# Second mixture of experts: sixteen tiles instead of eight go through all experts on chip, in two sets

## What is computed

```python
logits = ln(t) @ gate_w + gate_b                     # 16 experts
top_probs, top_idx = top_k(softmax(logits), 2)       # two of them, shares normalized
h = silu(ln(t) @ w1[e]) * (ln(t) @ w2[e])            # 64 -> 128
t = t + sum over the two chosen e of share[e] * (h @ w3[e])   # 128 -> 64
```

## Time and profile before

| | |
|---|---|
| median of 3 runs | 960.18 us (952.63, 961.45, 960.18) |
| profiled execution | 959.24 us, span 957.1 us |
| busy share of the span | TensorE 68%, VectorE 59%, GpSimd 54%, ScalarE 30% |
| mean granted TensorE clock | 0.787 of full speed |
| `stage_mixture` of the second mixture | 693.8 to 881.4 us of the span |
| `stage_out` | 882.4 to 957.1 us |

### The profile page before, as it was taken

The page is one execution under the profiler, slowest core; times in us unless marked ns, Lnnn a source line. Parts: engine busy times, 40 slices in busy tenths (PEclk is TensorE's granted clock), DMA queues, the critical chain, the costliest instruction groups (busy, mean ns, idle before and its releaser), DMA issues. The chain is left out here.

```text
span 957.1 us, 12138 instructions
## 1 busy us (share of the span) xinstructions
PE 646.1 (68%) x3571; PEld 429.6 (45%) x3571; DVE 568.5 (59%) x1058; ACT 288.4 (30%) x556; POOL 517.4 (54%) x494
## 2 busy tenths in 40 slices
PE   3797875405239989989519953199455998930893
PEld 2795863404223257767413443134243776720222
DVE  6468575597796523545676558854574553510685
ACT  1356225212213333445220021200213544510232
POOL 1063341330677777367477740777207747774774
PEclk9999996655559955989858975589756997975897
DMA  4000941000430112345281100000002434421813
GB/s 128 7 1 1 213 163 34 0 1 1 126 96 24 45 65 88 109 119 141 78 131 27 27 15 2 24 27 26 11 1 76 142 112 109 138 57 29 186 25 104
DMA packets 71104, 64.77 MB, mean 68 GB/s; under 512 B 22933, under 2 KB 58597, under 8 KB 71043
## 3 DMA queue, kind: packets, MB, share of 16 engines
q1 hardware_dynamic: 55272, 48.90, 18.8%
q0 software_dynamic: 14336, 14.71, 6.2%
q10 hardware_dynamic: 1435, 0.40, 0.2%
HBM read 36.57 MB, written 27.39 MB: 67 GB/s over the span
## 5 line engine op out<-in xcount | busy, mean ns | idle before, releaser
L1086 POOL DMA_INDIRECT gy<-blocks_y,L_ffnslot x224 | 221.1, 987 | 115.1 <-issue 67.5
L1074 POOL DMA_INDIRECT blocks_x<-L_ffnlxm,L_ffnslot x112 | 112.1, 1001 | 105.0 <-DVE L_ffnslot L1431 71.5
L1074 POOL DMA_INDIRECT blocks_x<-L_ffnmxm,L_ffnslot x112 | 117.6, 1050 | 72.3 <-DVE L_ffnslot L1431 38.5
L1460 DVE TENSOR_TENSOR L_ffnhid<-L_ffngate,L_ffnps 128x512 f32<-128x512 f32 x88 | 60.6, 688 | 109.9 <-ACT L_ffngate L1341 109.9
L1284 PE MATMUL L_ffnps<-L_ffnxc,L_ffnwr 64*128 64x256 f32 x704 | 115.0, 451 | 0.1
L1296 PEld LDWEIGHTS L_ffnps<-WR,L_ffnhid 128*128 128x128 f32 x704 | 92.5, 205 | 34.5 <-issue 34.5
L1296 PE MATMUL L_ffnps<-WR,L_ffnhid 128*128 x704 | 105.0, 296 | 2.3 <-DVE L_ffnhid L1460 2.3
L1284 PEld LDWEIGHTS L_ffnps<-L_ffnxc,L_ffnwr 64*128 64x128 f32 x704 | 68.8, 211 | 23.1 <-issue 17.0
L1680 PE MATMUL l_ps<-l_vg,l_pwb 128*128 128x512 f32 x128 | 68.3, 625 | 0.5 <-DVE l_vg L1792 0.5
L1792 DVE SCALAR_TENSOR_TENSOR l_vg<-l_ps,lw_bv,l_gain 128x512 f32<-128x512 f32 x64 | 44.7, 746 | 36.0 <-PE l_ps L1669 35.9
L1341 ACT ACTIVATE L_ffngate<-L_ffnps 128x512 f32<-128x512 f32 x88 | 52.5, 597 | 21.9 <-PE L_ffnps L1284 20.1
(11 more groups left out here) (312 smaller groups left out, 1260.4 us busy)
## 6 DMA issues: line engine op xcount, KB each, us to landing
L_ffnxb<-blocks_x SPq DMA_DIRECT2D x88, 128.0 KB
blocks_y<-L_ffnyb SPq DMA_DIRECT2D x88, 128.0 KB, 1.7
L_ffndbc<-shares SPq DMA_DIRECT2D x32, 256.0 KB, 8.5
blocks_x<-zeros SPq DMA_DIRECT2D x2, 3072.0 KB, 18.5
WR<-in_L_ffn_w SPq DMA_DIRECT2D x10, 512.0 KB, 10.0
gy<-blocks_y,L_ffnslot POOLq DMA_INDIRECT x224, 2.5
Xc<-in_x SPq DMA_DIRECT2D x4, 512.0 KB, 6.7
out_x<-o_y SPq DMA_DIRECT2D x8, 256.0 KB, 3.0
```

Source lines behind the costliest of these rows:

```text
L1074: pool.indirect_dma_start(self.XD[part], bass.IndirectOffsetOnAxis(self.slot[:, part, k, t:t + 1], 0), self.XN[part][:, t], None).then_inc ...
L1086: pool.indirect_dma_start(self.GY[part][:, k, t], None, self.YD[part][0:self.units[part] * UNIT * BS], bass.IndirectOffsetOnAxis(self.slot ...
L1460: dve.tensor_tensor(self.hid[:, n % 2].rearrange("p b s n -> p b (s n)"), self.gate[:, n % 2], ps[:, bank:bank + 2, BS:2 * BS], ALU.mult). ...
```

## The change

The second mixture gets `sets` = 2: its part 1 keeps 16 tiles on the routed way (16 units, 32 scatters, 32 gathers, in place of 20, 48 and 48), and 16 tiles go the dense way in two sets `z` of eight. Set 0 (tiles 48 to 55) is worked on in `stage_mixture`, behind the units of part 1; set 1 (tiles 56 to 63) in `stage_out` as before. The shares of both sets go out together in 8 DMAs. `shares_in` runs twice: for set 0 in `sync`, between the last store of part 0 and the first load of part 1, and for set 1 at the head of `stage_out`. `combine` of part 1 falls from three quarters to two; the order of the output groups becomes 7, 6, 0 to 5. With 16 tiles kept, the second group of part 1's counting (`tot`) is a memset in place of an add. The first mixture has `sets` = 1 as it was; only `own` now lies in the memory of `xs`, and `sq` in that of `dgate`, in both mixtures.

```diff
-        self.tiles = [TH - DT * (part == dense) for part in range(PARTS)]
+        self.tiles = [TH - DT * sets * (part == dense) for part in range(PARTS)]
...
@@ sync
                 if i >= 4:
                     store(part, i - 4)
+            if self.dense == 1 and part == 0:
+                self.shares_in(sp, 0)
...
@@ shares_out
-        for j in range(DT // 2):
-            sp.dma_start(self.DW[:, j, :], self.dwT[2 * E * j:2 * E * (j + 1), :]).then_inc(self.dw_stored, 16)
+        for z in range(self.sets):
+            for j in range(DT // 2):
+                sp.dma_start(self.DW[z, :, j, :], self.dwT[2 * E * j:2 * E * (j + 1), z]).then_inc(self.dw_stored, 16)
...
@@ shares_tensor
-        pe.transpose(self.ps[:, 7, 2 * P:3 * P], self.dw[:].rearrange("p t e -> p (t e)"), self.K["ident"][:]
-                     ).then_inc(self.dw_mm, 1)
+        for z in range(self.sets):
+            ins = pe.transpose(self.ps[:, 7, (2 + z) * P:(3 + z) * P],
+                               self.dw[:, z * DT:(z + 1) * DT].rearrange("p t e -> p (t e)"), self.K["ident"][:])
+        ins.then_inc(self.dw_mm, 1)
...
@@ tensor, for each part, behind its units
+            if self.dense == 1 and part == 1:
+                pe.wait_ge(self.xc_out, last)
+                pe.wait_ge(self.y_out, last)
+                self.dense_tensor(pe, 0, 0, E)
...
@@ scalar
+            if self.dense == 1 and part == 1:
+                self.dense_scalar(act, 0, E)
...
@@ vector
+            if self.dense == 1 and part == 1:
+                self.dense_vector(dve, then, 0, 0, E)
...
@@ stage_out
-        order = [Q // 2 - 1] + list(range(Q // 2 - 1))
+        order = [Q // 2 - 1, Q // 2 - 2] + list(range(Q // 2 - 2))
...
-                mix.dense_tensor(pe, 0, E)
+                mix.dense_tensor(pe, 1, 0, E)
...
-                    if n:
-                        pe.wait_ge(added, 4 * n)
+                    if n >= 2:
+                        pe.wait_ge(added, 4 * (n - 1))
...
-                mix.shares_in(sp)
+                mix.shares_in(sp, 1)
...
@@ build
-        mix2 = Mixture(nc, sem, ctx, A, K, X, "L3_ffn", WR, XD, YD, GY, 1, DW[1])
+        mix2 = Mixture(nc, sem, ctx, A, K, X, "L3_ffn", WR, XD, YD, GY, 1, 2, DW[1])
```

More of the change, by code:

```diff
@@ L920, with __init__ @@
 class Mixture:
-    def __init__(self, nc, sem, kept, A, K, X, L, WR, XD, YD, GY, dense, DW):
+    def __init__(self, nc, sem, kept, A, K, X, L, WR, XD, YD, GY, dense, sets, DW):
         def sb(name, shape, dt=F32):
@@ L989, in sems @@
             return [sem(self.L + n) for n in names]
-        self.dwT = sb("dwt", [P, P])
+        self.dwT = sb("dwt", [P, self.sets, P])
         self.xb = sb("xb", [P, 4, SB * C])
@@ L1112, in turned_tiles, with dense_tensor @@
     def turned_tiles(self, part, k):
-        return self.xd[:] if part == self.dense and k == 3 else self.XT[:, k]
+        z = k - 4 + self.sets
+        return self.xd[:, z] if part == self.dense and z >= 0 else self.XT[:, k]
     def shares_tensor(self, pe):
         pe.wait_ge(self.dw_ready, 1)
-        pe.transpose(self.ps[:, 7, 2 * P:3 * P], self.dw[:].rearrange("p t e -> p (t e)"), self.K["ident"][:]
-                     ).then_inc(self.dw_mm, 1)
+        for z in range(self.sets):
+            ins = pe.transpose(self.ps[:, 7, (2 + z) * P:(3 + z) * P],
+                               self.dw[:, z * DT:(z + 1) * DT].rearrange("p t e -> p (t e)"), self.K["ident"][:])
+        ins.then_inc(self.dw_mm, 1)
     def shares_scalar(self, act):
         act.wait_ge(self.dw_mm, 1)
-        act.copy(self.dwT[:], self.ps[:, 7, 2 * P:3 * P]).then_inc(self.dw_sb, 1)
-    def dense_tensor(self, pe, e0, e1):
+        act.copy(self.dwT[:].rearrange("p z t -> p (z t)"), self.ps[:, 7, 2 * P:(2 + self.sets) * P]).then_inc(self.dw_sb, 1)
+    def dense_tensor(self, pe, z, e0, e1):
         ps, WR = self.ps, self.WR
@@ L1141, in up @@
                             pe.wait_ge(self.dsilu, n - 2)
-                        x = self.xd[rows]
+                        x = self.xd[rows, z]
                     else:
@@ L1180, in dense_scalar, with dense_vector @@
         act.copy(self.yT[:], self.ps[:, 7, :]).then_inc(self.yt_sb, 1)
-    def dense_vector(self, dve, then, e0, e1, between=lambda e: None):
+    def dense_vector(self, dve, then, z, e0, e1, between=lambda e: None):
         def scaled(e):
@@ L1204, in dense_vector @@
         dve.wait_ge(self.yt_mm, 1)
-        t0 = self.dense * TH + TH - DT
+        t0 = self.dense * TH + TH - DT * (self.sets - z)
         x = self.X[:].rearrange("p q a (b c) -> p (q a b) c", b=2)[:, t0:t0 + DT].rearrange("p t c -> p (t c)")
@@ L1401, in route_vector @@
             ranked = slice(g * TG, min((g + 1) * TG, kept))
-            dve.tensor_tensor(self.tot[:, :, ranked].rearrange("p e t -> p t e"), self.one1[:, ranked], self.key[:, ranked],
-                              ALU.add).then_inc(self.counted, 1)
+            if g * TG < kept:
+                dve.tensor_tensor(self.tot[:, :, ranked].rearrange("p e t -> p t e"), self.one1[:, ranked], self.key[:, ranked],
+                                  ALU.add).then_inc(self.counted, 1)
+            else:
+                dve.memset(self.tot[:, :, tiles].bitcast(F32), 0.0).then_inc(self.counted, 1)
             dve.wait_ge(self.counted, n)
@@ L1508, in stage_mixture @@
         mix.blocks_room(st, sem)
-        if mix.dense == 0:
-            mix.dense_room(st, sem)
+        mix.dense_room(st, sem)
         if not first:
             mix.tiles_room(st, "m", range(PARTS))
-        mix.routing_room(st, "m", ps[:], sq=mix.dgate[:].rearrange("p (a k) t -> p a (k t)", a=2) if mix.dense == 0 else None)
+        mix.routing_room(st, "m", ps[:], sq=mix.dgate[:].rearrange("p (a k) t -> p a (k t)", a=2),
+                         own=mix.xs[:].rearrange("p a t -> p (a t)")[:, 0:NBLK * E].rearrange("p (n e) -> p n e", e=E))
         with nc.Block() as block:
@@ L1875, in early @@
                         mix.combine_quarter(dve, then, 0, e // 4)
-                mix.dense_vector(dve, then, 0, E, early)
+                mix.dense_vector(dve, then, 1, 0, E, early)
                 mix.combine(dve, then, PARTS - 1)
@@ L1911, in build @@
         YD = [nc.dram_tensor(f"blocks_y{h}", (NBLK * BS, C), F32, kind="Internal").ap() for h in range(PARTS)]
-        DW = [nc.dram_tensor(f"shares{k}", (2 * E, DT // 2, P), F32, kind="Internal").ap() for k in range(2)]
+        DW = [nc.dram_tensor(f"shares{k}", (k + 1, 2 * E, DT // 2, P), F32, kind="Internal").ap() for k in range(2)]
         zeroed, weights_in = nc.alloc_semaphore(name="zeroed"), nc.alloc_semaphore(name="weights_in")
```

31 lines of the change are left out of this document (15 added, 16 removed).

## The result

| | before | after |
|---|---|---|
| first comparison, median | 959.31 us (4 runs, 952.6 to 961.5) | 972.15 us (4 runs, 969.3 to 982.9) |
| ratio, 95% interval | | 1.017 (1.009 to 1.025) |
| second comparison, on another occasion | 951.72 us (23 runs) | 973.2 us (4 runs, 967.1 to 981.7) |
| ratio, 95% interval | | 1.025 (1.016 to 1.033) |
| profiled execution | 959.24 us, span 957.1 | 974.82 us, span 973.2 |

The medians are of all runs, the ratios of fast runs alone (those within 1.5% of the fastest run of the same kernel), so a ratio need not be the quotient of the medians. Both intervals lie above 1: the change makes the kernel slower, by 12.8 us of the medians in the first comparison and 21.5 us in the second. Whether the loss reaches 2% they leave open. The forecast was 982 in a range of 966 to 998, slower.

A forecast was written before the change was run, and what follows sets the result against it. Bounds: TensorE's pace in part 1's units, then GpSimd's gather and drain. The last stage begins 29.4 us later and shortens by 7.0: +22.4 on span 957.1 gives 979.5, time 981.6, 982.5 on the median; forecast 982, range 966 to 998.

The forecast's parts named there:

- Step 1: Shares out ahead of part 0's first load: 8 small DMAs instead of 4 and wider share operations, +2.1 us.
- Step 2: Between the parts: part 1's first load waits 22.1 us behind 16 broadcasts; TensorE starts 22.4 us later, shares out included.
- Step 3: Part 1 of the second mixture: four units fewer at 2.33 us each, -9.3 us.
- Step 4: Behind part 1's units in `stage_mixture`: the dense pass of set 0 takes 51 us (bounds 50 and 54).
- 5 the turn: From VectorE's end of the mixture stage to the last stage's first issue: 1.6 us, as in the first mixture.
- less the hole that was there before: Behind part 1's units: compute engines idle 35.2 us during GpSimd's gather and drain; the change puts the pass there.
- 6 the last stage: The last stage: unchanged dense pass bounds, then two quarters of combining and the tail; 67.7 us against 74.65, -7.0.
- The owner of the stage's end: End of the mixture stage: set by VectorE at 910.2 us, no longer by GpSimd, through at 883.4.
- Only the issue time: Rival, between the parts: broadcasts hold the load up only for their 10.1 us of issue; 972 us, chance 0.13.
- The pass fits the hole: Rival, mixture stage: part 1's loads are not held up, the pass ends at 889.9; 962 us, chance 0.09.
- A long stretch at low clock: Rival, part 1's restart: TensorE's clock stays low 41 us instead of 11, +12.5 us; 995 us, chance 0.13.
- The clock elsewhere: Rival, first mixture: its 41 us low-clock stretch can be missing, shifting single runs up to 17 us; faster by luck 0.03.

The follow-up runs named there:

- the quarter of the data: The changed kernel with set 0's 16 broadcasts at a quarter of the data each, same number of issues; one execution, 957.8 us.
- the late broadcasts: The changed kernel with set 0's 16 broadcasts issued behind part 1's last load, not between the parts; 953.1 us median, 0.999 of the kernel before.

## Why the prediction was right

Step by step, forecast beside measured in the profiled execution:

| step | forecast | measured |
|---|---|---|
| 1 shares out, mark to the first unit | +2.1 | 724.53 - 718.72 = 5.8 against 3.95: +1.9 (and 0.7 ahead of the mark) |
| part 0's 24 units | 0 | 62.9 against 61.1: +1.8 (clock back later) |
| 2 shares in | +20.3 | 23.3 against 2.2: +21.1 |
| 3 four units fewer | -9.3 | 42.6 against 54.35: -11.8 |
| 4 the pass | 51 | 853.61 to 903.16: 49.5 |
| 5 the turn | 1.6 | 1.6 |
| less the hole that was there before | -36.4 | 882.45 - 846.08 = 36.4 |
| last stage begins, against before | +29.4 | 904.8 - 718.7 - (882.45 - 724.0) = +27.6 |
| 6 the last stage | -7.0 | 68.4 against 74.65: -6.2 |
| sum behind the mark | +22.4 | +21.4 |

*Step 1* was forecast with the share operations in it; measured from the first of them it is +2.6, inside its bounds of 1.7 and 3.

*Step 2*, the largest, held in size and cause. The choice between 10.1 and 22.1 us was made for the data, and the quarter of the data shows both parts of it. The rule that was cited from the Trainium skill ("DMA: Bandwidth & Descriptors", "Queues, rings and completion order") says that each DMA engine consumes descriptors in ring order. The trace agrees: the first load could be used only 13.1 us after its own issue, behind the broadcasts on the same queue, and 3.1 us after it with a quarter of the data ahead.

*Step 3* gave 2.5 us more than the four units, where TensorE's clock was back 6 us after the restart and not 11. *Step 4* was over by 1.5 us: it began at full clock, where the one of the first mixture began low.

*The owner of the stage's end* changed as said. The pass makes the stage 25 us longer, which the runs without it show directly.

*The sum's size* is shown for one execution. The second trace of the changed kernel, at +17.9 behind the mark and 0.7 ahead of it, lies 3.8 us under the forecast, so part of the close agreement of the first is luck.

*The rivals.* "Only the issue time" (972) meets the first median to the microsecond and is wrong all the same: the idle time was 24.1, not 13 us. "The pass fits the hole" (962) is what the late broadcasts show: with the hold-up gone the medians stand 1.4 us apart and the ratio is 0.999, where +2.1 us was worked out. "A long stretch at low clock" in part 1 did not come in the changed kernel's traces, but in both of the late broadcasts', with 41 and 28.5 us: two of the twelve traces, which does not speak against the 0.13 that it had been given. Its price was sized well: 41 us low in place of 6 cost 15.6 us. "The clock elsewhere" had the right mechanism and too small a place: it is the likeliest source of the 10 us by which the median missed the forecast. The forecast was laid on a profiled execution with the 41 us stretch and both traces of the changed kernel had the short one, so -6 to -10 was to be had from that alone; I treated it as scatter about the median when it was a property of the one execution on which the sum was laid.

What stays open: why the clock comes back after 6 us in one restart and after 41 in another of the same code. No run here varied that alone.

## To carry to other kernels

A hole on the compute engines is worth only what fits between the work that precedes it and the engine that sets its end: a 49.5 us pass put behind units into a 35 us hole costs 25 us once its own inputs have held those units up by 21. Place bulk transfers on a shared queue behind the last small load that somebody waits for: the same 4.2 MB cost 21 us between the parts, some 10 among part 0's units, and nothing behind part 1's last load. And when a total moves by 1 to 2%, compare from a mark behind which the change lies; the totals here differed by 10 us with the clock's draw in a stage that nobody had touched.

## What was not expected of the hardware

A small load behind bulk transfers waits for them even though its own issue is quick: four loads of 128 KB were issued in 1.94 us behind 4.2 MB of broadcasts, and the first could be used 13.1 us after its issue, against 2.2 us with nothing ahead and 3.1 us behind a quarter of the data. In the meantime GpSimd's gathers, which the page lists under a queue of their own (q0, the loads and broadcasts under q1), hardly slowed: the gather of part 0 took 82.2 us against 80.4.

TensorE's clock stayed at 1.2 GHz for 41 us in a stretch in which TensorE was busy all the time, and for 10 us at the same place in other executions (342.9 to 353.1 in the changed kernel). After restarts behind a 3 us gap it came back in 6 to 41 us.
